# Expert weights worked on during the first batch's attention, in the token tiles' memory

## Chip, cores and metric

The kernel runs on one core of one Trainium2 chip. The metric is the device time of one launch in microseconds (us), lower is better. Engines are called PE (TensorE), DVE (VectorE), ACT (ScalarE), POOL (GpSimd) and SP (SyncE).

## What is computed

Two batches of 2048 tokens of width 256 pass through attention with 4 heads of 64, and then through a layer in which each token goes through one of 8 expert matrices. Cut to what matters:

```python
x = x + _layernorm(attn(_layernorm(x), ln_gamma, ..., w_q, w_k, w_v, w_o, b_o))
# attn: layernorm, q/k/v projections, rmsnorm of q and k, softmax(q k^T) v, w_o
x = x + _layernorm(ffn(_layernorm(x), gate_w, expert_w))

def ffn(x, gate_w, expert_w):
    scores = jnp.einsum('bsh,eh->bse', x, gate_w)
    onehot = jax.nn.one_hot(jnp.argmax(scores, axis=-1), 8)
    expert_out = jnp.einsum('bsh,efh->bsef', x, expert_w)
    return x + jnp.einsum('bsef,bse->bsf', expert_out, onehot)
```

## The kernel before

For each batch there is a front, an attention and an output stage; behind both batches comes the expert stage.

**Front.** 16 token tiles of 128, in groups of 4. Each group gets its statistics (L765, L768) and is normalised (L777) on DVE, transposed on PE (L1191), split into a high and a low part (L481 ACT, L784 DVE) and projected on PE (L1206, L1209, L1154). Then each tile's q and k are squared, summed, scaled and split (L487 and L509 ACT; L788, L796, L799, L807, L815, L818 DVE; L385, L389 POOL) and transposed (L1223, L1226).

**Attention.** 128 steps: 4 heads, 2 blocks of 1024 queries, 16 key tiles. In step s PE makes the scores of 128 keys against 1024 queries (L1300) in one of three PSUM slots; ACT takes the exponential (L574) into one of 6 buffers; POOL issues a DMA that casts it to 16 bits (L412), in most steps (ACT does the cast in one step of 8, at L580, and DVE does the last few); DVE subtracts the cast from the exponential to get the low part (L941); PE multiplies high and low with v (L1318 to L1320), six steps later. PE's order is fixed by hand: the scores of steps k and k+1, then the products of steps k-6 and k-5. The scores of step s wait for the exponential of step s-3, and the exponential of step s for the subtraction of step s-6. Two of the six exponential buffers are the upper half of `x_all`, the memory of the token tiles; its tiles 8 to 15 are therefore loaded again behind the attention (L293), while tiles 0 to 7 stay until the residual (L993).

**Expert weights.** 8 experts by 2 halves of the input features make 16 pieces w of 128 x 256. Each piece passes through four engines: `add_identity` (L354, POOL) adds the identity to its diagonal block, `expert_mean` (L824 and L826, DVE) finds the mean of each row, `high_expert` (L496, ACT) subtracts it and rounds to the high part, and `low_expert` (L360 and L362, POOL) makes the low part. Each waits for the one before it through a semaphore. In this kernel they are loaded in one DMA of 2 MB (L446) into `attn_x1`, the memory that will later take the heads' outputs, and 16 pieces are spread over the first batch's front: piece w is given its mean behind tile w+1, its high part by ACT behind tile w+2, its low part by POOL behind tile w+3. The last mean, the last three high parts and the last three low parts fall into the attention's first eleven steps. `move_out` of the first block waits for all 16 low parts, since it writes `attn_x1`.

**Order.** Every engine runs its own list in program order; a wait at the head holds everything behind it. On ACT, `head_act` runs `exp_step` and then what is hung on the step. On DVE, `head_dve` runs `parts` (the wait for the cast, and L941) and then what is hung on the step. On POOL, what is hung on step s stands ahead of the cast of step s.

Of the kernel before, what the change touches and what calls it, by code (L numbers as in the profile page):

```python
# [6 lines left out]
def build(nc, x, wqkvT, woT, weT, wgT, ln_gamma, ln_beta, q_gamma, k_gamma, b_o, out):  # L7
    f32, f32r, f16, u32 = mybir.dt.float32, mybir.dt.float32r, mybir.dt.float16, mybir.dt.uint32
    ALU, ACT, AX = mybir.AluOpType, mybir.ActivationFunctionType, mybir.AxisListType
    P = 128  # L10
    NB, N, D = x.shape
# [34 lines left out]
    with ExitStack() as ctx:  # L46
# [143 lines left out]

        raw_we = attn_x1[:, 0:KH * NE * D].rearrange("p (k n) -> p k n", k=KH)
        raw_q = q_T[:, :].bitcast(f32)
# [13 lines left out]
        s_rt = [sem(f"s_rt{i}") for i in range(NRT)]  # L206
        s_o = [sem(f"s_o{i}") for i in range(NOT)]
        s_cast = [sem(f"s_cast{i}") for i in range(NHI)]

        s_id, s_ones, s_wf, s_qg, s_q2 = sems("id ones wf qg q2")  # L210

        s_xr, s_tid, s_wI, s_wr, s_wl2 = sems("xr tid wI wr wl2")

# [47 lines left out]
        def dma_casts(s):  # L261
            return not act_casts(s) and not dve_casts(s)

        def casts(by, s):
            return sum(by(i) for i in range(s + 1))
# [7 lines left out]
        def _(sp):  # L273
# [12 lines left out]
            sp.wait_ge(s_tid, TIDS)  # L286
            sp.dma_start(rows_d.rearrange("(s p) w -> p s w", p=P).bitcast(u32), spread(absent[:, :], 1, NSL)).then_inc(s_init, 16)

            for b in range(0, NB):
# [20 lines left out]
        def _(pool):  # L310
# [33 lines left out]
            def half_expert(w):  # L344
                e, k = w // KH, w % KH
                return raw_we[:, k, e * D:(e + 1) * D]

            def add_identity(w):
                k = w % KH
                if w == 0:  # L350
                    pool.wait_ge(s_we, 16)
                    pool.wait_ge(s_id, 4)
                diagonal = half_expert(w)[:, k * P:(k + 1) * P]
                pool.tensor_tensor(diagonal, diagonal, ident[:, :], ALU.add).then_inc(s_wI, 1)  # L354

            def low_expert(w):
                e, k = w // KH, w % KH
                half, cols = half_expert(w), slice(e * D, (e + 1) * D)
                pool.wait_ge(s_weh, w + 1)
                pool.tensor_tensor(half, half, wmean[:, w:w + 1].to_broadcast([P, D]), ALU.add).then_inc(s_wr, 1)  # L360
                pool.wait_ge(s_wr, w + 1)
                pool.tensor_tensor(we_l[:, k, cols], half, we_h[:, k, cols].bitcast(f32), ALU.subtract).then_inc(s_wl2, 1)  # L362
# [15 lines left out]
            for b in range(0, NB):  # L378
                for gi in range(0, NG):
                    for t in range(TG):  # L380
                        n = (b * NG + gi) * TG + t
                        qn = qk_n[t % 2][:, 0:D]
                        qv = qn.rearrange("p (h d) -> p h d", h=H)
                        pool.wait_ge(s_qkn, n + 1)
                        pool.tensor_tensor(qv, qv, spread(gq[:, :], 1, H), ALU.mult).then_inc(s_qg, 1)  # L385
                        pool.wait_ge(s_qg, n + 1)
                        if n > 0:
                            pool.wait_ge(s_qs, n)
                        pool.tensor_tensor(q_sq[:, :], qn, qn, ALU.mult).then_inc(s_q2, 1)  # L389
                        if n == 0:  # L390
                            pool.wait_ge(s_wh, KH + 2)
                            pool.tensor_tensor(wo_l[:, :, 0:D], raw_wo, wo_h[:, :, 0:D].bitcast(f32), ALU.subtract).then_inc(s_wf, 1)
                        if b == 0:
                            add_identity(n)
                        if b == 0 and n >= 3:
                            low_expert(n - 3)
                        if b:
                            scatter_tile(b - 1, n % NT)
                for s in range(b * ALL, (b + 1) * ALL):
                    if 8 <= s < 11:  # L400
                        low_expert(NT - 11 + s)
                    if s == b * ALL + 2:
                        pool.wait_ge(s_T2, b * NT + NT - 1)
                    if s == b * ALL + 3:
                        pool.wait_ge(s_qs, b * NT + NT)
                    if dma_casts(s):
                        pool.wait_ge(s_E, s + 1)
                        if s - NHI + 1 > 0:
                            pool.wait_ge(s_PV, s - NHI + 1)
                        if s < NHI:  # L410
                            pool.wait_ge(s_init, 16)
                        pool.dma_start(high[s % ALL % NHI], whole[s % ALL % NEF]).then_inc(s_cast[s % ALL % NHI], 16)  # L412
# [17 lines left out]
        def _(act):  # L430
# [6 lines left out]
            def prepare():  # L437
# [6 lines left out]
                for k in range(KH):  # L444
                    act.activation(wqkv_h[:, k, 0:3 * D], raw_wqkv[:, k, :], ACT.Copy, scale=gam[:, k:k + 1]).then_inc(s_wh, 1)
                act.dma_start(raw_we, weT.rearrange("(k p) n -> p k n", p=P)).then_inc(s_we, 16)  # L446
                act.wait_ge(s_wgc, 1)
# [23 lines left out]
            for b in range(0, NB):  # L471
# [21 lines left out]
                def high_expert(w):  # L493
                    e, k = w // KH, w % KH
                    act.wait_ge(s_wm, 2 * w + 2)
                    act.activation(we_h[:, k, e * D:(e + 1) * D], raw_we[:, k, e * D:(e + 1) * D], ACT.Identity,  # L496
                                   bias=wmean[:, w:w + 1]).then_inc(s_weh, 1)
# [29 lines left out]
                def a_act(gi, first=False, last=False):  # L527
                    g = b * NG + gi
                    for t in range(TG):
# [9 lines left out]
                        if n == 1:  # L539
                            gate_of_output()  # L540
                        if b == 0 and 2 <= n < NT - 1:
                            high_expert(n - 2)
                        if t == 2 and not last:
# [41 lines left out]
                def head_act(b, h):  # L585
                    hh = b * H + h
                    for k in range(STEPS):
# [4 lines left out]
                        if h == 0 and k == 1:  # L592
                            move_k(end - 1, NT - 1)
                        if b == 0 and h == 0 and k in (5, 6, 7):
                            high_expert(NT - 8 + k)

# [90 lines left out]
        def _(dve):  # L687
# [73 lines left out]
            for b in range(0, NB):  # L761
# [59 lines left out]
                def expert_mean(w):  # L821
                    e, k = w // KH, w % KH
                    dve.wait_ge(s_wI, w + 1)
                    dve.tensor_reduce(wesum[:, w:w + 1], raw_we[:, k, e * D:(e + 1) * D], AX.X, ALU.add).then_inc(s_wm, 1)  # L824
                    dve.wait_ge(s_wm, 2 * w + 1)
                    dve.tensor_scalar(wmean[:, w:w + 1], wesum[:, w:w + 1], -1.0 / D, None, ALU.mult).then_inc(s_wm, 1)  # L826

                def a_dve(gi, first=False, last=False):
                    g = b * NG + gi
                    for t in range(TG):  # L830
# [5 lines left out]
                        if n == 1:  # L836
                            gate_of_output()
                        if b == 0 and n >= 1:
                            expert_mean(n - 1)
                        if not (first and t < 1):  # L840
# [102 lines left out]
                def move_out(h, qb):  # L943
                    unit = (b * H + h) * NQB + qb
                    dve.wait_ge(s_PV, unit * NT + NT)
                    if unit == b * H * NQB and b:
                        dve.wait_ge(s_sc, b * NT * 16)
                    if unit == 0:
                        dve.wait_ge(s_wl2, NE * KH)
                    inverse = rl[:, unit % 2, :].rearrange("p (b q) -> p b q", b=2)  # L950
# [6 lines left out]
                def head_dve(b, h):  # L957
                    hh = b * H + h
                    for k in range(STEPS):
# [5 lines left out]
                        if h == 0 and k == 0:  # L965
                            largest_out(1)
                        if b == 0 and h == 0 and k == 2:
                            expert_mean(NT - 1)
                        if h == 0 and k == 4:
# [15 lines left out]
                def residual(i):  # L985
                    pr = b * NP + i
                    dve.wait_ge(s_r1, pr + 1)
                    dve.reciprocal(rs1[:, i % 2, :], sd1[:, i % 2, :]).then_inc(s_k1, 1)
                    dve.wait_ge(s_k1, pr + 1)
                    if 2 * i == XT:  # L990
                        dve.wait_ge(s_xr, (b + 1) * (NEF - 4) * 16)
# [479 lines left out]
```

## Time and profile before

| | us |
|---|---|
| median of 3 runs | 762.37 |
| lowest, highest | 761.49, 763.06 |
| profiled execution | 765.08 |
| its span, first to last instruction | 763.4 |
| front of batch 0, up to its first exponential | 0 to 108.9 |
| attention of batch 0, up to the last block's move | 108.9 to 314 |
| first exponential of batch 1 | 435.5 |

A line of the trace names an instruction's place in the code (L574), its engine, what it writes and reads, how many there were, and its times. What stands in brackets, or behind a bar, is the time that the engine was idle just before, and what ended it.

### The profile page before, as it was taken

To read this page: it belongs to the slowest core of one execution; us is meant where nothing else is said; L and a number is where in the kernel's file an instruction comes from. 1 tells how busy PE (TensorE), PEld (TensorE's weight loads), DVE (VectorE), ACT (ScalarE), POOL (GpSimd) and SP (SyncE) were. 2 spreads that over 40 slices of the span, in tenths; PEclk is the share of its full clock that TensorE was granted. 3 is DMA by queue.
4 is the path that set the end of the run, shared out by engine and by line. 5 is a ranking of instruction groups with operands and counts; after the bars stand their busy time and mean duration, and the time that the engine had idled before them with its cause. 6 is when DMAs were issued, how large, how long until landed. Compare 5 with 4: busy or idle time off the path is not lost.

```text
span 763.4 us, 22051 instructions
## 1 busy us (share of the span) xinstructions
PE 656.3 (86%) x8914; PEld 447.4 (59%) x8914; DVE 607.0 (80%) x1169; ACT 538.4 (71%) x866; POOL 271.9 (36%) x454
## 2 busy tenths in 40 slices
PE   4988878999999999867999899999999998706882
PEld 2666544566666656755766556666666567505772
DVE  4799978878887888896887777888887888963884
ACT  3278788888888878582677988888888785713552
POOL 2245565232332322000555622323323220071775
PEclk9589999999999999996898899999999999956997
DMA  7910006997979878121000178879798781024551
GB/s 251 270 37 1 1 17 113 169 162 142 166 144 163 154 144 151 57 69 44 29 29 22 45 133 156 161 141 167 145 163 153 141 153 58 3 96 135 175 164 44
DMA packets 53815, 87.13 MB, mean 114 GB/s; under 512 B 6608, under 2 KB 23250, under 8 KB 53460
## 3 DMA queue, kind: packets, MB, share of 16 engines
q0 software_dynamic: 34848, 65.61, 44.7%
q1 hardware_dynamic: 18020, 18.03, 8.4%
q10 hardware_dynamic: 848, 2.10, 0.8%
q8 instruction: 71, 1.16, 0.7%
q14 instruction: 28, 0.23, 0.1%
HBM read 14.82 MB, written 14.79 MB: 39 GB/s over the span
## 4 chain that ended last, share of the span: by engine, by line
PE 50%; DVE 22%; DMA 10%; ACT 8%; issue 7%; POOL 1%; SPq 0%; POOLq 0%; DVEq 0%; ACTq 0%
PE banks L1300 13%; PE banks L1154 12%; DVE e_l L941 6%; PE banks L1318 5%; DMA e_h<-e_f 5%; PE banks L1319 5%; PE banks L1206 4%; PE banks L1320 4%; DMA e_x<-x_all 4%; ACT e_f L574 2%; DVE x_all L993 1%; PE banks L1191 1%; PE banks L1422 1%; PE banks L1209 1%; ACT x_all L574 1%
## 5 line engine op out<-in xcount | busy, mean ns | idle before, releaser
L941 DVE TENSOR_TENSOR e_l<-e_f,e_h 128x1024 f16<-128x1024 f32 x172 | 207.7, 1230 | 40.5 <-DMA e_h<-e_f 37.5
L574 ACT ACTIVATE e_f<-banks,nbias,c_ 128x1024 f32<-128x1024 f32 x172 | 199.0, 1200 | 44.6 <-PE banks L1300 44.6
L1300 PE MATMUL banks<-q_T,k_T 128*128 128x512 f16 (+1 forms) x1024 | 204.5, 384 | 4.8 <-DVE e_l L807 3.2
L1320 PE MATMUL banks<-v_mm,e_l 128*128 128x65 f16 x2048 | 201.8, 191 | 0.0
L1320 PEld LDWEIGHTS banks<-v_mm,e_l 128*128 128x128 f16 x2048 | 189.6, 99 | 0.0
L1318 PEld LDWEIGHTS banks<-v_mm,e_h 128*128 128x128 f16 x1376 | 126.0, 96 | 44.2 <-issue 24.9
L1318 PE MATMUL banks<-v_mm,e_h 128*128 128x65 f16 x1376 | 136.7, 193 | 9.2 <-DVE e_l L941 4.3
L412 POOL DMA_DIRECT2D e_h<-e_f x148 | 78.5, 530 | 175.7 <-ACT e_f L574 170.1
L1319 PE MATMUL banks<-v_mm,e_h 128*128 128x64 f16 x1376 | 136.2, 195 | 0.0
L1319 PEld LDWEIGHTS banks<-v_mm,e_h 128*128 128x128 f16 x1376 | 127.2, 97 | 0.0
L941 DVE TENSOR_TENSOR e_l<-x_all,e_x 128x1024 f16<-128x1024 f32 x84 | 101.7, 1227 | 21.2 <-DMA e_x<-x_all 17.7
L574 ACT ACTIVATE x_all<-banks,nbias,c_ 128x1024 f32<-128x1024 f32 x84 | 97.5, 1201 | 21.3 <-PE banks L1300 19.9
L1300 PEld LDWEIGHTS banks<-q_T,k_T 128*128 128x128 f16 (+1 forms) x1024 | 55.9, 96 | 94.3 <-issue 58.0
L1318 PEld LDWEIGHTS banks<-v_mm,e_x 128*128 128x128 f16 x672 | 61.5, 96 | 20.2 <-issue 11.0
L1318 PE MATMUL banks<-v_mm,e_x 128*128 128x65 f16 x672 | 66.9, 193 | 2.7 <-DVE attn_x L955 1.8
L1319 PE MATMUL banks<-v_mm,e_x 128*128 128x64 f16 x672 | 66.6, 195 | 0.0
L412 POOL DMA_DIRECT2D e_x<-x_all x70 | 37.0, 528 | 82.0 <-ACT x_all L574 73.9
L1319 PEld LDWEIGHTS banks<-v_mm,e_x 128*128 128x128 f16 x672 | 62.1, 97 | 0.0
L385 POOL TENSOR_TENSOR e_l<-e_l,gq 128x256 f32<-128x256 f32 x32 | 28.5, 889 | 87.9 <-DVE e_l L807 87.9
L426 POOL DMA_INDIRECT out<-k_T x40 | 39.5, 988 | 30.4 <-DVE k_T L1135 23.1
L487 ACT ACTIVATE e_f<-banks 128x512 f32<-128x512 f32 x32 | 19.1, 596 | 33.3 <-PE banks L1154 30.3
L374 POOL DMA_INDIRECT rows_d<-attn_x,rowat x32 | 31.8, 994 | 29.0 <-DVE ttab L1082 18.2
(268 smaller groups left out, 1237.4 us busy)
## 6 DMA issues: line engine op xcount, KB each, us to landing
e_h<-e_f POOLq DMA_DIRECT2D x148, 256.0 KB, 3.9
e_x<-x_all POOLq DMA_DIRECT2D x70, 256.0 KB, 4.0
x_all<-x SPq DMA_DIRECT2D x12, 512.0 KB, 4.4
rows_d<-e_x SPq DMA_DIRECT2D x1, 5180.0 KB, 24.4
k_T<-rows_d SPq DMA_DIRECT2D x20, 259.0 KB, 3.1
attn_x<-weT ACTq DMA_DIRECT2D x1, 2048.0 KB, 7.6
q_T<-wqkvT SPq DMA_DIRECT2D x1, 768.0 KB, 6.2
out<-k_T POOLq DMA_INDIRECT x40, 2.7
```

The lines of the kernel that those rows point to most:

```text
L374: pool.indirect_dma_start(out=rows_d, out_offset=bass.IndirectOffsetOnAxis(ap=rowat[:, b * NT + i:b * NT + i + 1], axis=0), in_=x1_all[:, ...
L385: pool.tensor_tensor(qv, qv, spread(gq[:, :], 1, H), ALU.mult).then_inc(s_qg, 1)
L412: pool.dma_start(high[s % ALL % NHI], whole[s % ALL % NEF]).then_inc(s_cast[s % ALL % NHI], 16)
L426: pool.indirect_dma_start(out=out_rows, out_offset=bass.IndirectOffsetOnAxis(ap=rt[q % NRT][:, t, D + 2:D + 3].bitcast(u32), axis=0), in_= ...
L574: act.activation(whole[s % ALL % NEF], ps_S[s % ALL % 3], ACT.Exp, bias=bias_of(h, k // NT), scale=CESC).then_inc(s_E, 1)
L941: dve.tensor_tensor(low[s % ALL % NLO], whole[s % ALL % NEF], high[s % ALL % NHI], ALU.subtract).then_inc(s_El, 1)
L1154: ins = pe.matmul(dst, l, r, start=(i == 0), stop=(i == n - 1))
L1206: pe.matmul(ps_QK[t % 2], l, r, start=i == 0, stop=False)
L1300: ins = pe.matmul(ps_S[s % ALL % 3][:, c * BANK:(c + 1) * BANK], k_T[rows, 1 - c if cross else c, h * N + j * P:h * N + (j + 1) * P], q_T[ ...
L1318: pe.matmul(o, high[s % ALL % NHI][:, at], v[:, 0:DH + 1], start=first, stop=False, skip_group_check=True)
L1319: pe.matmul(o[:, 0:DH], high[s % ALL % NHI][:, at], v[:, DH + 1:VW], start=False, stop=False, skip_group_check=True)
L1320: ins = pe.matmul(o, low[s % ALL % NLO][:, at], v[:, 0:DH + 1], start=False, stop=j == NT - 1, skip_group_check=True)
```

## The change

The expert weights move out of `attn_x1` and out of the front. `x_all[:, 0:8]` has been normalised for the first batch by then, and nobody reads it until the residual. It takes experts 0 to 3 (two DMAs by SP, issued once eight tiles have been normalised), then experts 4 to 7 one by one as places come free, and then the eight token tiles again, one by one (eight DMAs), before the first residual, which waits for them. The work on piece w is hung on steps of the first batch's attention: with s = 4 + 7w, POOL adds the identity ahead of the cast of step s; DVE makes the mean behind the subtraction of step s; ACT makes the high part behind the exponential of step s+2; POOL makes the low part in two halves, ahead of the casts of steps s+4 and s+5. The ACT-issued load of 2 MB and `move_out`'s wait for the low parts are gone.

```diff
-        raw_we = attn_x1[:, 0:KH * NE * D].rearrange("p (k n) -> p k n", k=KH)
+        WSLOTS = NT // 2 // KH
+        raw_we = x_all[:, 0:KH * WSLOTS, :].rearrange("p (k e) d -> p k e d", k=KH)
...
+        def expert_at(s):
+            first, every = 4, 7
+            if s >= first and (s - first) % every == 0 and (s - first) // every < NE * KH:
+                return (s - first) // every
+            return None
...
+            weT_k = weT.rearrange("(k p) (e d) -> p k e d", p=P, d=D)
+            sp.wait_ge(s_xh, KH * WSLOTS)
+            for k in range(KH):
+                sp.dma_start(raw_we[:, k], weT_k[:, k, 0:WSLOTS]).then_inc(s_we, 16)
+            for e in range(WSLOTS, NE):
+                sp.wait_ge(s_wl2, KH * (e - WSLOTS + 1))
+                sp.dma_start(raw_we[:, :, e - WSLOTS, :], weT_k[:, :, e]).then_inc(s_wx[e - WSLOTS], 16)
+            for e in range(WSLOTS, NE):
+                sp.wait_ge(s_wl2, KH * (e + 1))
+                for k in range(KH):
+                    at = k * WSLOTS + e - WSLOTS
+                    sp.dma_start(x_all[:, at, :], x_d[:, at, :]).then_inc(s_xw, 16)
...
             def add_identity(w):
-                k = w % KH
+                e, k = w // KH, w % KH
+                if e < WSLOTS:
+                    pool.wait_ge(s_we, 16 * KH)
+                else:
+                    pool.wait_ge(s_wx[e - WSLOTS], 16)
...
                 pool.tensor_tensor(half, half, wmean[:, w:w + 1].to_broadcast([P, D]), ALU.add).then_inc(s_wr, 1)
+
+            def lowest_expert(w):
+                e, k = w // KH, w % KH
+                half, cols = half_expert(w), slice(e * D, (e + 1) * D)
                 pool.wait_ge(s_wr, w + 1)
                 pool.tensor_tensor(we_l[:, k, cols], half, we_h[:, k, cols].bitcast(f32), ALU.subtract).then_inc(s_wl2, 1)
...
-                        if b == 0:
-                            add_identity(n)
-                        if b == 0 and n >= 3:
-                            low_expert(n - 3)
...
-                    if 8 <= s < 11:
-                        low_expert(NT - 11 + s)
+                    for part, lag in ((add_identity, 0), (low_expert, 4), (lowest_expert, 5)):
+                        w = expert_at(s - lag)
+                        if w is not None:
+                            part(w)
...
-                act.dma_start(raw_we, weT.rearrange("(k p) n -> p k n", p=P)).then_inc(s_we, 16)
...
-                        if b == 0 and 2 <= n < NT - 1:
-                            high_expert(n - 2)
...
-                        if b == 0 and h == 0 and k in (5, 6, 7):
-                            high_expert(NT - 8 + k)
+                        if expert_at(hh * STEPS + k - 2) is not None:
+                            high_expert(expert_at(hh * STEPS + k - 2))
...
-                        if b == 0 and n >= 1:
-                            expert_mean(n - 1)
...
-                    if unit == 0:
-                        dve.wait_ge(s_wl2, NE * KH)
...
-                        if b == 0 and h == 0 and k == 2:
-                            expert_mean(NT - 1)
+                        if expert_at(hh * STEPS + k) is not None:
+                            expert_mean(expert_at(hh * STEPS + k))
...
+                    if pr == 0:
+                        dve.wait_ge(s_xw, KH * WSLOTS * 16)
```

## Rows read from the trace of the kernel before

**Rows 1.** The page: busy us and share of each engine; granted clock in 40 slices
```profile
PE 656.3 (86%) x8914; PEld 447.4 (59%) x8914; DVE 607.0 (80%) x1169; ACT 538.4 (71%) x866; POOL 271.9 (36%) x454
...
PEclk9589999999999999996898899999999999956997
```
**Rows 2.** Busy time by stretch: us, PE, PEld, DVE, ACT, POOL, clock, DMA share, GB/s
```profile
32.00:42.00 10.00, 10.00 (x42) 7.28 (x43) 6.80 (x18) 4.82 (x13) 2.50 (x4) 0.64 0.96 239
...
45.70:106.60 60.90, 50.60 (x329) 36.22 (x328) 58.43 (x142) 48.91 (x113) 36.39 (x60) 0.97 0.00 1
...
376.30:433.20 56.90, 52.71 (x329) 38.29 (x328) 47.02 (x118) 43.98 (x102) 32.35 (x36) 0.91 0.08 27
...
377.50:383.86 6.36, 4.81 (x40) 3.56 (x39) 5.82 (x20) 4.69 (x13) 3.86 (x5) 1.00 0.06 21
383.86:387.28 3.42, 3.42 (x10) 2.00 (x7) 3.35 (x9) 2.49 (x6) 0.87 (x2) 0.50 0.00 0
...
404.30:411.20 6.90, 6.90 (x29) 5.17 (x28) 4.62 (x13) 4.28 (x11) 3.35 (x4) 0.51 0.12 41
...
149.61:246.41 96.80, 95.37 (x1794) 60.59 (x1792) 79.09 (x76) 80.28 (x73) 29.56 (x56) 1.00 0.85 154
```
**Rows 3.** Groups of instructions in batch 0's front, 45.7 to 106.6 us: busy, mean ns
```profile
L824 DVE TENSOR_REDUCE wesum<-attn_x 128x1 f32<-128x256 f32 x12 | 4.9, 408 | 0.0
...
L815 DVE TENSOR_TENSOR e_l<-e_l 128x512 f16<-128x512 f32 x6 | 6.1, 1017 | 0.0
...
L777 DVE TENSOR_SCALAR e_h<-x_all,mv,rs 128x256 f32<-128x256 f32 x8 | 5.3, 728 | 0.1
...
L496 ACT ACTIVATE we_h<-attn_x,wmean 128x256 fp32r<-128x256 f32 x11 | 5.5, 499 | 0.0
```
**Rows 4.** The same groups in batch 1's front, 376.3 to 433.2 us
```profile
L815 DVE TENSOR_TENSOR e_l<-e_l 128x512 f16<-128x512 f32 x6 | 4.1, 680 | 0.0
...
L777 DVE TENSOR_SCALAR e_h<-x_all,mv,rs 128x256 f32<-128x256 f32 x8 | 3.4, 481 | 0.1
```
**Rows 5.** One line's instructions: durations ns min/median/max; the casts' landing below L412
```profile
L354 POOL TENSOR_TENSOR attn_x<-attn_x,ident x16: 454/458/508, 29.5 to 109.7; 128x128 f32<-128x128 f32 x16
...
L362 POOL TENSOR_TENSOR we_l<-attn_x,we_h x16: 722/726/1601, 50.3 to 130.7; 128x256 fp32r<-128x256 f32 x16
...
L360 POOL TENSOR_TENSOR attn_x<-attn_x,wmean x16: 607/613/1032, 49.6 to 129.6; 128x256 f32<-128x256 f32 x16
...
L412 POOL DMA_DIRECT2D e_x<-x_all x70: 527/527/565, 119.0 to 618.6; - x70
...
DMA to landing us min/median/max: 2.8/4.0/5.7
```
**Rows 6.** Exponentials counted in stretches: us, ACT busy (count), clock, DMA share, GB/s
```profile
149.60:246.40 96.80, 73.50 (x64) 1.00 0.85 154
108.90:124.60 15.70, 9.38 (x8) 0.89 0.57 104
124.60:136.80 12.20, 9.21 (x8) 1.00 0.64 117
435.50:450.00 14.50, 9.01 (x8) 0.78 0.63 118
```
**Rows 7.** Timeline, ACT, POOL and DVE: one step of the attention (step 33)
```profile
162.62 1.05 ACT L580 ACTIVATE e_h<-e_f 128x1024 f16<-128x1024 f32 x1
163.57 1.19 ACT L574 ACTIVATE e_f<-banks,nbias,c_ 128x1024 f32<-128x1024 f32 x1
164.66 2.29 ACT L574 ACTIVATE x_all<-banks,nbias,c_ 128x1024 f32<-128x1024 f32 x2
167.47 2.30 ACT L574 ACTIVATE e_f<-banks,nbias,c_ 128x1024 f32<-128x1024 f32 x2 [0.52 <-PE banks L1300]
...
165.06 0.53 POOL L412 DMA_DIRECT2D e_h<-e_f  x1 [1.46 <-ACT e_f L574]
...
169.44 1.22 DVE L941 TENSOR_TENSOR e_l<-e_f,e_h 128x1024 f16<-128x1024 f32 x1 [1.13 <-DMA e_h<-e_f]
```
**Rows 8.** Timeline, where the last pieces lie in batch 0's attention today
```profile
120.53 0.41 DVE L824 TENSOR_REDUCE wesum<-attn_x 128x1 f32<-128x256 f32 x1
120.97 0.15 DVE L826 TENSOR_SCALAR wmean<-wesum 128x1 f32<-128x1 f32 x1
...
122.78 0.50 ACT L496 ACTIVATE we_h<-attn_x,wmean 128x256 fp32r<-128x256 f32 x1
123.17 1.19 ACT L574 ACTIVATE e_f<-banks,nbias,c_ 128x1024 f32<-128x1024 f32 x1
...
127.45 1.60 POOL L362 TENSOR_TENSOR we_l<-attn_x,we_h 128x256 fp32r<-128x256 f32 x1
...
128.38 6.10 DVE L941 TENSOR_TENSOR e_l<-e_f,e_h 128x1024 f16<-128x1024 f32 x4
```
**Rows 9.** Who waited for whom, 136 to 290 us: total us, times, longest
```profile
ACT e_f L574 <- PE banks L1300: 18.2, 25, 1.9
...
DVE e_l L941 <- DMA e_h<-e_f: 15.7, 16, 1.8
```
**Rows 10.** Timeline of the start: ACT's load of the weights, SP's store of empty rows
```profile
9.51 0.39 ACTq L446 DMA_DIRECT2D attn_x<-weT  x1
...
18.73 0.51 SPq L287 DMA_DIRECT2D rows_d<-e_x  x1
```
**Rows 11.** The page: DMA issues, KB each, us to landing
```profile
rows_d<-e_x SPq DMA_DIRECT2D x1, 5180.0 KB, 24.4
...
attn_x<-weT ACTq DMA_DIRECT2D x1, 2048.0 KB, 7.6
```
**Rows 12.** Timeline, DVE: the first residual of batch 0
```profile
319.00 0.88 DVE L993 SCALAR_TENSOR_TENSOR x_all<-banks,rs,x_all 128x256 f32<-128x256 f32 x2
```

More of the change, by code:

```diff
@@ L207, in build @@
         s_o = [sem(f"s_o{i}") for i in range(NOT)]
+        s_wx = [sem(f"s_wx{i}") for i in range(NE // 2)]
         s_cast = [sem(f"s_cast{i}") for i in range(NHI)]
         s_id, s_ones, s_wf, s_qg, s_q2 = sems("id ones wf qg q2")
-        s_xr, s_tid, s_wI, s_wr, s_wl2 = sems("xr tid wI wr wl2")
+        s_xr, s_xw, s_tid, s_wI, s_wr, s_wl2 = sems("xr xw tid wI wr wl2")
         s_prep, s_const, s_ws, s_woc, s_wgc, s_bc, s_wm, s_b2, s_bq, s_wl = sems("prep const ws woc wgc bc wm b2 bq wl")
@@ L345, in half_expert @@
                 e, k = w // KH, w % KH
-                return raw_we[:, k, e * D:(e + 1) * D]
+                return raw_we[:, k, e % WSLOTS, :]
             def add_identity(w):
-                k = w % KH
+                e, k = w // KH, w % KH
[3 more added lines that the diff above has]
+                    pool.wait_ge(s_wx[e - WSLOTS], 16)
                 if w == 0:
-                    pool.wait_ge(s_we, 16)
                     pool.wait_ge(s_id, 4)
@@ L495, in high_expert @@
                     act.wait_ge(s_wm, 2 * w + 2)
-                    act.activation(we_h[:, k, e * D:(e + 1) * D], raw_we[:, k, e * D:(e + 1) * D], ACT.Identity,
+                    act.activation(we_h[:, k, e * D:(e + 1) * D], raw_we[:, k, e % WSLOTS, :], ACT.Identity,
                                    bias=wmean[:, w:w + 1]).then_inc(s_weh, 1)
@@ L823, in expert_mean @@
                     dve.wait_ge(s_wI, w + 1)
-                    dve.tensor_reduce(wesum[:, w:w + 1], raw_we[:, k, e * D:(e + 1) * D], AX.X, ALU.add).then_inc(s_wm, 1)
+                    dve.tensor_reduce(wesum[:, w:w + 1], raw_we[:, k, e % WSLOTS, :], AX.X, ALU.add).then_inc(s_wm, 1)
                     dve.wait_ge(s_wm, 2 * w + 1)
```

## Prediction

> **What bounds the kernel now.** I read the page first: PE is busy 86%, DVE 80%, ACT 71% [rows 1]. That is an average over stages, so the next view is the busy time by stretch. In batch 0's front, from 45.7 to 106.6 us (tiles 3 to 15), DVE is busy 58.4 of 60.9 us and PE 50.6: DVE sets the pace there. The same twelve tiles of batch 1 take 56.9 us with DVE busy only 47.0 [rows 2]; batch 1 has no expert pieces, so it is a measured picture of batch 0's front without them. Before that, at 32 to 42 us, PE is busy 10.0 of 10 us at a clock of 0.64 and DVE 6.8 [rows 2], so nothing taken from DVE helps there. In the attention PE is busy 95.4 of 96.8 us [rows 2]; 64 exponentials start in these 96.8 us [rows 6], which is 1.51 us a step and 10.6 us for seven. DVE and ACT are busy 79 and 80 us of it. They have room on average; what matters for this change is the order in which they meet, so the last view is the timeline of one step.
>
> **The front.** Removed per piece on DVE: L824 0.41 and L826 0.15 us, 0.56 in sequence [rows 3, 8]; on ACT L496 0.50; on POOL three operations. Beside it, what is left becomes shorter: L815 takes 1.02 us in batch 0 and 0.68 in batch 1, and L777 0.73 and 0.48 [rows 3, 4], where POOL works on no pieces. Twelve pieces give 6.7 us of DVE time, the L815 rows 2.0 and L777 2.0: some 10.7 of 58.4, more than the path can give back, since PE and ACT come next. The bounds come from batch 1: 60.9 - 56.9 = 4.0 us as measured. But batch 1's stretch has 10.3 us at a clock of 0.5 (two stretches [rows 2]), in which PE did half the work, and batch 0's 3.4 us; the difference of 6.9 us at half speed is 3.5 us, which makes 7.5. The three tiles before may add up to 3.1 (their time over that of batch 1's, in a stretch that PE fills): 10.6 at most. I take **-6.5**, between 4.0 and 10.6 and nearest to 7.5, since the clock may fall in the new front as in batch 1's.
>
> **The start.** The 2 MB load at 9.51 us [rows 10] goes. The transfers that the start waits for have landed by then, and later ones are needed long after: 0 us. The new load of 1 MB stands on SP's queue behind the 5180 KB store [rows 10], issued at 18.7 us and landing 24.4 us later, so at 43; with 7.6 us for twice as much [rows 11] it is there by about 50, and step 4 comes after 108: 0 us. If the cover were gone, it would cost its landing time, at most 7.6.
>
> **The attention, order of work.** This is the step that decides. Take the trace of step 33 [rows 7]: its exponential ends at 164.76; POOL issues the cast at 165.06; it has landed when DVE starts L941 at 169.44, which ends at 170.66. The exponential of step 36, three steps later, starts at 167.47. So DVE finishes a step 5.9 us after its exponential, and by then ACT has been at the exponential of step s+3 for 3.2 us. The change hangs the mean on DVE behind L941 of step s, and lets ACT, behind the exponential of step s+2, wait for this mean. ACT waits in order: behind that wait stand L496 and the exponentials of all later steps, and behind those PE's scores, POOL's casts and in the end DVE itself. The wait cannot be met in time in any step for which POOL issues the cast.
>
> From the end of the exponential of step s to the start of that of step s+3:
> - 0.3 to the cast's issue [rows 7], 4.0 from there to its landing (2.8 at the least, 5.7 at most [rows 5]), 1.2 for L941 [rows 7];
> - 0.6 for L824 and L826; L496 starts and is through 0.4 later, as far as the next exponential is concerned (122.78 to 123.17) [rows 8].
>
> Sum 6.5, against 3.3 on average today (three steps less one exponential of 1.2). Then come the exponentials of steps s+3 to s+7, as fast as ACT can: four starts 1.1 apart and 1.2 for the last [rows 7], 5.6 us, and half of ACT's cast of 1.05 every eight steps: 0.5. Step s+7 is the next s. One round is 6.5 + 5.6 + 0.5 = 12.6 us; I add 0.3 because in every other round PE can't give the scores of s+7 that early (it must do two products between pairs of scores), and 0.4 for POOL's pieces: 13.3, against 10.6. **+2.7 a round.** For 15 rounds (pieces 1 to 15): 40.5. PE can't win this back between stalls, since its 95.4 of 96.8 us are its own work. Nor can casts run ahead, since the same stall holds them.
>
> Piece 0 takes the place of the last mean, three high and three low parts, which lie in the first steps now; batch 0's first eight steps took 15.7 us and batch 1's 14.5 [rows 6]. A gain of 1 and a charge of about 1: 0.
>
> Bounds of a round: with landings of 2.8 and none of the additions 6.5 - 1.2 + 5.6 + 0.5 = 11.4, or +0.8; with 5.7, 15.0, or +4.4. For 15 rounds +12 to +66. I take 4.0 because DMA share is 0.85 today [rows 2], and ACT's exponentials, and so the casts, come in bursts 1.1 apart after each stall.
>
> **POOL's pieces.** L354 0.46, L360 0.61 and L362 0.73 us alone [rows 5] are 1.8 us a round on an engine that is busy 29.6 of 96.8 us [rows 2]. What they do to others shows where they lie in the attention now: L362 stretches to 1.60 and four L941 take 6.10 us instead of 4.9 [rows 8], 0.3 each. Once or twice a round, that is the 0.4 above. The Trainium skill (SBUF — State Buffer, Who interferes with whom) says that a DVE instruction with two SBUF inputs and a GpSimd instruction that reads SBUF shut each other out for the whole of an instruction. By that rule a round could lose up to 1.8 us on DVE, where the row has 0.3 an instruction; on the path, fifteen times 1.8 would add 27 us, and I follow the row.
>
> **Clock.** In batch 1's front the clock went to 0.5 at 383.86, after a stretch in which PE was busy 4.81 of 6.36 us, or 76% [rows 2]. In the new rounds PE is busy 10.5 of 13.3 us, or 79%, so falls are likely. Each of 3.4 us costs PE 1.7 us of work, but most of that lies in PE's own new idle time. Between 0 and 13 (eight falls, fully paid) I take **+4**.
>
> **The rest.** Twelve loads, 2 MB in all, run beside the casts; alone 2 MB took 7.6 us [rows 11], the bound of their cost; their effect is within the landing that I took: 0. `add_identity` stands ahead of the cast of step s while POOL still waits for the exponential: 0. SP's own queue: the reloads of tiles 8 to 15 and the next batch's tiles now stand behind the last low part at step 114; they wait for step 124 anyway: 0. The first residual at 319.0 [rows 12] waits for tiles whose last load is issued about step 114, some 28 us earlier, and takes about 4: 0, and at most 4 without cover. `move_out`'s lost wait was met at step 11, before step 18: 0.
>
> **Sum.** -6.5 + 40.5 + 4 = +38. The profiled execution took 765.1, which would become 803.1; it stands 2.7 above the median of the runs, so on their scale 762.4 + 38 = **800.4**.
>
> **Rivals.**
> - *The stall is mostly caught up.* Landings near 2.8 (the queue is empty after a stall) and no clock falls: -10.6 + 12 gives 764, and from there to 776. For it: two of three PSUM slots can be full when ACT resumes. Against: casts in a burst queue. 8%.
> - *Faster.* Buffers absorb the wait. ACT waits for PE 18.2 us in 154 in one of its two groups alone [rows 9]; if this room and the three PSUM slots carried ACT over, only the front's gain would stay: 762.4 - 6.5 = 755.9. It decides if the mean is there within about 2 us of the end of the exponential of s+2, and the row says 3 or more. The Trainium skill (Perfetto Trace Analysis, Optimization Strategy) says that where the most-contended engine changes over time, interleaving the regimes may help; by that rule DVE work would leave a front that DVE bounds for an attention that PE bounds, for this same 756. The rows of busy time agree with it, the timeline of order does not. 6%.
> - *The clock stays down* for much of the attention. At half speed a round of PE's own work takes 21 us instead of 10.6; over a quarter of the rounds that is +40 more, 840. 6%.
> - *Forecast*, one stall a round: 80%.
>
> **How the numbers follow.** The forecast's own ends are 776 (rounds at +1.3, the front at -6.5, no clock cost) and 828 (rounds at +4.4, the front at -4, the clock at +4); the range is these, with 8% below, 6% faster and 6% above left out. What a measurement can tell from no change is 0.2%, 1.5 us. Faster by more: 6%. Within 0.2%: 2%, out of the first rival. Slower: 92%.
>
> **What would show it.** In the profile after, ACT's L496 should have idle time before it, some 3 us, fifteen times, ended by DVE's L826; L574's wait for PE should shrink; PE should have new idle time at L1300, ended by ACT's L574; exponentials should come in bursts of four or five 1.1 us apart with a gap behind them; a stretch of 64 should take about 122 us instead of 96.8. The front of batch 0 should reach its first exponential near 102 instead of 108.9, with L815 at 0.68 us. L496 without idle time before it, or the exponentials still 1.51 apart, would prove the forecast wrong; a residual that waits for a DMA would be a mistake in the part on the rest.

## The result

The change is slower: 802.9 us (798.6 to 808.1) against 762.7 (761.5 to 765.2); the ratio is 1.051, with an interval of 1.047 to 1.055. The forecast was 800.4. The profiled execution took 804.7 us, with a span of 803.0.

Line numbers have moved: L574 is now L597 (exponential), L941 L962 (subtraction), L412 L438 (cast), L1300 L1321 (scores), L1318 to L1320 L1339 to L1341 (products), L496 L521 (high part), L824 and L826 L847 and L849 (mean), L354, L360 and L362 L378, L384 and L390 (POOL's pieces), L815 L838, L777 L800.

The start times of the first exponential and of that of step 120 in each batch cut the two executions into stages (us; "behind" is everything behind batch 1's step 120):

| | to first exponential | batch 0's attention | between | batch 1's attention | behind |
|---|---|---|---|---|---|
| before | 108.9 | 186.5 | 140.1 | 184.5 | 143.4 |
| the change | 99.2 | 236.6 | 139.5 | 184.6 | 143.1 |
| difference | -9.7 | +50.1 | -0.6 | +0.1 | -0.3 |

The whole loss is in the first batch's attention. Busy time in this stage, before and (second row) in the change (us, PE, PEld, DVE, ACT, POOL, clock, DMA share, GB/s):

```profile
108.90:295.37 186.47, 178.70 (x3243) 110.89 (x3239) 152.48 (x159) 153.48 (x143) 64.11 (x115) 0.99 0.82 149
```

```profile
99.16:335.70 236.54, 195.70 (x3234) 118.26 (x3231) 161.38 (x187) 158.41 (x155) 92.14 (x154) 0.92 0.68 126
```

The page of the profile after, its clock row and the groups that changed:

```profile
PE 671.5 (84%) x8914; PEld 453.4 (56%) x8914; DVE 602.6 (75%) x1169; ACT 537.9 (67%) x866; POOL 284.8 (35%) x454
...
PEclk9699988999999999999599889999999999965997
...
L1321 PE MATMUL banks<-q_T,k_T 128*128 128x512 f16 (+1 forms) x1024 | 214.2, 394 | 41.5 <-ACT e_f L597 26.9
...
L521 ACT ACTIVATE we_h<-x_all,wmean 128x256 fp32r<-128x256 f32 x16 | 8.1, 508 | 53.3 <-DVE wmean L849 53.3
```

The last row says it in one line: 16 high parts, 8.1 us of work, and 53.3 us in which ACT stood still for the means. DVE and ACT do no more work in all than they did [rows 1]. Who waited for whom in the changed attention, 108 to 330 us (total us, times, longest):

```profile
ACT we_h L521 <- DVE wmean L849: 53.3, 16, 5.4
...
PE banks L1321 <- ACT e_f L597: 26.4, 17, 4.2
DVE e_l L962 <- DMA e_x<-x_all: 17.7, 14, 3.7
ACT e_f L597 <- PE banks L1321: 16.1, 15, 2.2
...
DVE e_l L962 <- PE banks L1341: 13.9, 7, 2.9
```

In [rows 9] ACT waited for PE. It still does, but less (22.6 us in both its groups over this stage, 31.6 before), and now PE waits for ACT, at the scores. One such round, as the chain of waits goes through it (start, us, what):

```profile
205.01 0.52 POOL x_all L378
205.53 5.73 DMA e_x<-x_all
...
211.35 1.23 DVE e_l L962
212.58 0.34 DVE wesum L847
...
212.94 0.17 DVE wmean L849
...
213.54 1.19 ACT e_f L597
```

And the same moment in the timelines of ACT and PE:

```profile
205.88 2.30 ACT L597 ACTIVATE e_f<-banks,nbias,c_ 128x1024 f32<-128x1024 f32 x2 [0.68 <-PE banks L1321]
213.13 0.51 ACT L521 ACTIVATE we_h<-x_all,wmean 128x256 fp32r<-128x256 f32 x1 [4.95 <-DVE wmean L849]
213.54 1.19 ACT L597 ACTIVATE e_f<-banks,nbias,c_ 128x1024 f32<-128x1024 f32 x1
...
214.78 1.59 PE L1321 MATMUL banks<-q_T,k_T 128*128 128x512 f16 x6 [3.74 <-ACT e_f L597]
```

This is step 53, whose exponential ended at 205.20. ACT has finished the exponential of step 55 at 208.18 and can do nothing until the mean behind step 53's subtraction is there. PE has filled its three slots and stands for 3.7 us. It is the chain that the forecast drew from step 33 [rows 7]: exponential, cast, subtraction, mean, high part, next exponential.

### The profile page after: what moved, and what is told of

Read it like the earlier page. It is cut to its first block, busy times and chain, and to the rows that moved or that the text cites. A ratio compares the mean times of both kernels' runs of the same rounds, so it can differ in the third digit from the quotient of the medians.

```text
span 803.0 us, 22064 instructions
## 1 busy us (share of the span) xinstructions
PE 671.5 (84%) x8914; PEld 453.4 (56%) x8914; DVE 602.6 (75%) x1169; ACT 537.9 (67%) x866; POOL 284.8 (35%) x454
## 4 chain that ended last, share of the span: by engine, by line
PE 32%; DVE 18%; DMA 12%; ACT 10%; issue 9%; POOL 2%; POOLq 0%; ACTq 0%; DVEq 0%
PE banks L1175 9%; DVE e_l L962 9%; PE banks L1321 8%; DMA e_h<-e_f 7%; DMA e_x<-x_all 4%; ACT e_f L597 4%; PE banks L1339 3%; PE banks L1227 3%; PE banks L1340 3%; PE banks L1341 2%; ACT x_all L597 2%; DVE x_all L1014 1%; PE banks L1443 1%; ACT e_h L603 1%; PE banks L1247 1%
## 5 line engine op out<-in xcount | busy, mean ns | idle before, releaser
L962 DVE TENSOR_TENSOR e_l<-e_f,e_h 128x1024 f16<-128x1024 f32 x172 | 210.2, 1244 | 64.9 <-DMA e_h<-e_f 49.1
L1321 PE MATMUL banks<-q_T,k_T 128*128 128x512 f16 (+1 forms) x1024 | 214.2, 394 | 41.5 <-ACT e_f L597 26.9
L597 ACT ACTIVATE e_f<-banks,nbias,c_ 128x1024 f32<-128x1024 f32 x172 | 198.8, 1199 | 39.3 <-PE banks L1321 39.3
L1341 PE MATMUL banks<-v_mm,e_l 128*128 128x65 f16 x2048 | 209.5, 194 | 0.0
L1341 PEld LDWEIGHTS banks<-v_mm,e_l 128*128 128x128 f16 x2048 | 194.1, 101 | 0.0
L1339 PEld LDWEIGHTS banks<-v_mm,e_h 128*128 128x128 f16 x1376 | 128.5, 97 | 42.0 <-issue 27.8
L1339 PE MATMUL banks<-v_mm,e_h 128*128 128x65 f16 x1376 | 141.1, 195 | 6.3 <-DVE e_l L962 4.3
L438 POOL DMA_DIRECT2D e_h<-e_f x148 | 79.5, 537 | 188.2 <-ACT e_f L597 178.5
L1340 PE MATMUL banks<-v_mm,e_h 128*128 128x64 f16 x1376 | 140.6, 197 | 0.0
L1321 PEld LDWEIGHTS banks<-q_T,k_T 128*128 128x128 f16 (+1 forms) x1024 | 55.5, 97 | 140.1 <-issue 62.7
L1340 PEld LDWEIGHTS banks<-v_mm,e_h 128*128 128x128 f16 x1376 | 129.8, 98 | 0.0
L962 DVE TENSOR_TENSOR e_l<-x_all,e_x 128x1024 f16<-128x1024 f32 x84 | 103.3, 1249 | 31.4 <-DMA e_x<-x_all 25.9
L597 ACT ACTIVATE x_all<-banks,nbias,c_ 128x1024 f32<-128x1024 f32 x84 | 97.6, 1199 | 18.4 <-PE banks L1321 17.0
L1339 PEld LDWEIGHTS banks<-v_mm,e_x 128*128 128x128 f16 x672 | 63.4, 98 | 19.7 <-issue 13.1
L413 POOL TENSOR_TENSOR e_l<-e_l,gq 128x256 f32<-128x256 f32 x32 | 34.7, 1086 | 108.5 <-DVE e_l L830 108.5
L1339 PE MATMUL banks<-v_mm,e_x 128*128 128x65 f16 x672 | 70.0, 196 | 1.5 <-DVE attn_x L974 1.2
L1340 PE MATMUL banks<-v_mm,e_x 128*128 128x64 f16 x672 | 69.7, 198 | 0.0
L438 POOL DMA_DIRECT2D e_x<-x_all x70 | 37.5, 535 | 86.6 <-ACT x_all L597 78.7
L1340 PEld LDWEIGHTS banks<-v_mm,e_x 128*128 128x128 f16 x672 | 64.0, 99 | 0.0
L452 POOL DMA_INDIRECT out<-k_T x40 | 39.6, 991 | 30.1 <-DVE k_T L1156 22.4
L521 ACT ACTIVATE we_h<-x_all,wmean 128x256 fp32r<-128x256 f32 x16 | 8.1, 508 | 53.3 <-DVE wmean L849 53.3
## 6 DMA issues: line engine op xcount, KB each, us to landing
x_all<-weT SPq DMA_DIRECT2D x2, 512.0 KB, 12.3
```

The lines of the kernel that those rows point to most:

```text
L452: pool.indirect_dma_start(out=out_rows, out_offset=bass.IndirectOffsetOnAxis(ap=rt[q % NRT][:, t, D + 2:D + 3].bitcast(u32), axis=0), in_= ...
L597: act.activation(whole[s % ALL % NEF], ps_S[s % ALL % 3], ACT.Exp, bias=bias_of(h, k // NT), scale=CESC).then_inc(s_E, 1)
L962: dve.tensor_tensor(low[s % ALL % NLO], whole[s % ALL % NEF], high[s % ALL % NHI], ALU.subtract).then_inc(s_El, 1)
L1321: ins = pe.matmul(ps_S[s % ALL % 3][:, c * BANK:(c + 1) * BANK], k_T[rows, 1 - c if cross else c, h * N + j * P:h * N + (j + 1) * P], q_T[ ...
L1339: pe.matmul(o, high[s % ALL % NHI][:, at], v[:, 0:DH + 1], start=first, stop=False, skip_group_check=True)
L1340: pe.matmul(o[:, 0:DH], high[s % ALL % NHI][:, at], v[:, DH + 1:VW], start=False, stop=False, skip_group_check=True)
```

## The experiments

The stage that they are read from is batch 0's attention, from its first exponential to that of step 120: 186.5 us before, 236.6 in the change. Each is one profiled execution; the unchanged copy of the kernel before took 187.4, and a second profile of the kernel with ACT's part at s+6 took 190.0 where the first had 188.7. So a difference of about 1 us in this stage tells nothing. Every time of a whole kernel is compared with runs of the kernel before on the same chip. The experiments ran in three series, each on a chip of its own. On two of these chips the kernel before itself took 780 to 781 us, on the third 763.8: its unchanged copy on one of the two had nearly the same stages up to batch 1's step 120 (620.3 us in all, against 620.0), and the expert stage took 160.8 in place of 143.4.

**1. Take ACT's wait away, leave everything else.**

```diff
                 pool.wait_ge(s_weh, w + 1)
+                pool.wait_ge(s_wm, 2 * w + 2)
...
-                    act.wait_ge(s_wm, 2 * w + 2)
+                    act.wait_ge(s_wI, w + 1)
...
-                                   bias=wmean[:, w:w + 1]).then_inc(s_weh, 1)
+                                   bias=eps[:, 0:1]).then_inc(s_weh, 1)
```

> All instructions of the change stay; ACT's high part no longer waits for DVE's mean (it takes a constant as bias and waits for POOL's identity only, so the experts are not centred). Theory A (the cost is ACT's in-order wait for a mean that stands behind the cast): the stall goes, the attention of batch 0 from its first exponential to that of step 120 falls from 236.5 us back to 187 to 195, and with the front's 9.7 us gained the whole takes 753 to 762 us. Rival B (the cost is the added work of DVE and POOL on shared engines and the loads beside the casts): the attention stays above 215 us and the whole above 782. Rival C (the clock's falls are a cause of their own): the falls stay at about one in 27 us and the whole is near 785.

Ratio to before 1.011 (1.001 to 1.020), where A had expected a kernel no slower than before. Busy time from the first exponential to that of step 120 (us, PE, PEld, DVE, ACT, POOL, clock, DMA share, GB/s):

```profile
101.72:303.65 201.93, 180.53 (x3235) 111.76 (x3233) 169.21 (x186) 159.72 (x155) 102.34 (x154) 0.99 0.79 147
```

ACT's wait cost 34.7 us (236.6 to 201.9), most of the loss. But 15.4 us were left, where A had expected 8.5 at the most, so A as stated fell short. B's floor of 215 is not reached either. C is refuted as a cause of its own: with the stall gone the clock fell once in this stage, for 3.4 us, in place of nine times. The waits of this run, whose lines stand one further down, name the rest:

```profile
POOL x_all L385 <- DVE wmean L850: 26.6, 12, 5.3
```

With ACT no longer held, POOL gets to its low part (step s+4) before the mean is there; it now stands still, up to 5.3 us, with casts behind it. The same wait has moved to another engine.

**2. Take both waits away.** ACT as above; POOL takes the constant too, and the wait that experiment 1 gave it is not there. DVE's two instructions stay, on a finished weight.

```diff
-                pool.tensor_tensor(half, half, wmean[:, w:w + 1].to_broadcast([P, D]), ALU.add).then_inc(s_wr, 1)
+                pool.tensor_tensor(half, half, eps[:, 0:1].to_broadcast([P, D]), ALU.add).then_inc(s_wr, 1)
...
-                    dve.tensor_reduce(wesum[:, w:w + 1], raw_we[:, k, e % WSLOTS, :], AX.X, ALU.add).then_inc(s_wm, 1)
+                    dve.tensor_reduce(wesum[:, w:w + 1], wo_h[:, k, 0:D].bitcast(f32), AX.X, ALU.add).then_inc(s_wm, 1)
```

> As the run without ACT's wait, and POOL doesn't wait for the mean either: DVE's two mean instructions stay but read a finished weight, ACT and POOL take a constant (the experts are not centred). All positions and amounts of work are those of the change. Theory A, refined (in order waits for the mean are the cost on ACT and on POOL, where the low part of step s+4 stands ahead of a cast): batch 0's attention from its first exponential to that of step 120 takes 187 to 192 us, where the run without ACT's wait had 201.9 and the one with everything six steps later 188.7. Rival B (where POOL's pieces lie, right ahead of casts four and five steps on, disturbs by itself): it stays at 198 to 202.

```profile
99.28:288.04 188.76, 178.63 (x3234) 111.19 (x3231) 169.11 (x188) 158.74 (x155) 98.45 (x154) 0.99 0.85 158
```

188.8 us, and a ratio of 0.992 (0.987 to 0.997): a little faster than before. All the work of the change, at its places, with its loads and reloads, costs some 2 us; the waits for the mean, with everything that follows from them, the clock's falls included, cost the other 48. B is out.

**3. Only move POOL's parts, four steps later (s+8 and s+9).**

```diff
-                    for part, lag in ((add_identity, 0), (low_expert, 4), (lowest_expert, 5)):
+                    for part, lag in ((add_identity, 0), (low_expert, 8), (lowest_expert, 9)):
```

> The change with ACT as it is (step s+2, with its wait) and POOL's two halves moved from s+4 and s+5 to s+8 and s+9. If the two waits cost apart (ACT 34.7 of the 50.1 us, POOL 13.2), batch 0's attention falls from 236.6 to 222 to 226 us. If ACT's stall alone sets the rounds, since POOL's wait is met by then anyway (ACT resumes only when the mean is there), it stays at 233 to 237 us.

```profile
101.98:343.20 241.22, 196.30 (x3233) 117.96 (x3230) 167.72 (x188) 158.62 (x156) 100.50 (x154) 0.92 0.66 123
```

241.2 us, ratio 1.061 (1.050 to 1.071): no gain. The two waits don't add. In the change POOL never waits for the mean: no such line is in its view of waits. Its wait appears, and costs 13.1 us (201.9 less 188.8), only once ACT's is gone. That it is 4.6 us over the change's 236.6 was not expected; each is one profiled execution, and I did not follow it up.

**4. Make the same work wait for nothing: a longer distance.** In each, ACT's part is hung on step s+L, and POOL's on s+L+2 and s+L+3. This one is L = 6:

```diff
-                    for part, lag in ((add_identity, 0), (low_expert, 4), (lowest_expert, 5)):
+                    for part, lag in ((add_identity, 0), (low_expert, 8), (lowest_expert, 9)):
...
-                        if expert_at(hh * STEPS + k - 2) is not None:
-                            high_expert(expert_at(hh * STEPS + k - 2))
+                        if expert_at(hh * STEPS + k - 6) is not None:
+                            high_expert(expert_at(hh * STEPS + k - 6))
```

> The same with ACT's high part at step s+6 and POOL's halves at s+8 and s+9. Theory A: ACT reaches the wait 9.0 us after the exponential of step s, later than every mean seen: no stall, exponentials of seven steps in 10.6 to 11.2 us, whole 753 to 762 us, so at or below the kernel before. Rival B: 795 or more.

> ACT's high part is hung on step s+4 in place of s+2, POOL's two halves on s+6 and s+7; nothing else. Theory A: the mean is there 5.7 to 7.9 us after the end of the exponential of step s, and ACT reaches the wait after 6.0 us in place of 3.0, so a stall of 0 to 2 us is left in a part of the rounds: 765 to 778 us. Rival B: the work is the same, so the time stays within 5 us of 803.

> ACT's high part at step s+3, POOL's halves at s+5 and s+6. The stretch from batch 0's first exponential to that of step 120 took 236.6 us at s+2, 202.0 at s+4 and 188.7 at s+6. If a round costs what the mean is late (step s+3 gives ACT one exponential, 1.2 us, and one step's distance of 1.5 us more, 15 times): 236.6 less 18 to 23, so 214 to 219 us. If the cost were one of having the wait at all, whatever its distance: 230 or more.

| ACT's part at step | attention, us | idle before the 16 high parts, us | ratio to before |
|---|---|---|---|
| s+2 (the change) | 236.6 | 53.3 | 1.051 |
| s+3 | 211.7 | 37.6 | 780.3 us against 763.8, one execution |
| s+4 | 202.0 | 24.5 | 1.016 (1.009 to 1.022) |
| s+6 | 188.7, again 190.0 | 0 | 0.994 (0.991 to 0.998) |

The row of s+6:

```profile
102.02:290.72 188.70, 178.43 (x3238) 111.08 (x3235) 170.04 (x187) 158.54 (x156) 99.78 (x154) 0.99 0.85 157
```

POOL never waits for the mean in these three, so the table shows ACT's wait alone. One step is worth 24.9 us, the next 9.7: the cost falls with the distance, and B's "same time within 5 us" is refuted again. At s+3 the stretch ended a little below the expected 214 to 219. At s+4 the whole kernel was 12 us slower than before, so 776 on the scale of 763.8: inside the 765 to 778 expected. At s+6 the wait is always met, and the calculation is complete again: this kernel is faster than the kernel before and than the change. The same kernel once more, on another chip:

> The kernel with ACT at s+6 again, for its time alone. By the stages of the profiles it gains 7.4 us in the front and gives back 2 in the attention: 5.4 us, a ratio of 0.993; 0.994 was measured. If that was chance, the ratio is 0.998 or more.

Ratio 0.994 (0.991 to 0.997): 759.2 us against 763.8. Both intervals lie below 1, so the gain of 4.6 us is clear of noise, though small.

**5. What do the pieces disturb when nobody waits?** The kernel of L = 6 without POOL's low parts; the loads into freed places then wait for the high parts.

```diff
-                    for part, lag in ((add_identity, 0), (low_expert, 8), (lowest_expert, 9)):
+                    for part, lag in ((add_identity, 0),):
```

> The kernel with ACT at s+6, without POOL's low parts (L384, L390 left out; the expert stage takes the high weights in their place). If POOL's instructions hold up DVE's subtraction, its mean in batch 0's attention falls from 1.357 us to below 1.26, and the stretch from 188.7 to 186 to 187 us. If it is the mean and the identity that cost, it stays at 188 to 189.

Subtractions of batch 0's attention, with the low parts and (second fence) without (busy us, mean ns, idle before):

```profile
L962 DVE TENSOR_TENSOR e_l<-e_f,e_h 128x1024 f16<-128x1024 f32 x78 | 103.7, 1365 | 8.2 <-DMA e_h<-e_f 7.0 <-PE banks L1341 0.9
...
L390 POOL TENSOR_TENSOR we_l<-x_all,we_h 128x256 fp32r<-128x256 f32 x16 | 17.3, 1080 | 0.5
```

```profile
L962 DVE TENSOR_TENSOR e_l<-e_f,e_h 128x1024 f16<-128x1024 f32 x78 | 94.8, 1245 | 13.4 <-DMA e_h<-e_f 13.0
```

The subtraction falls from 1.37 to 1.25 us (1.39 in the second profile at s+6). POOL's operations do hold DVE up, 0.12 us on the mean of 116 subtractions or 14 us in all, but DVE has room for most of that: the stretch took 187.1 us, 1.6 and 2.9 less than the two profiles at s+6. That is little more than these two differ by themselves, and the ratios of the whole overlap (0.989, 0.981 to 0.996, against 0.994), so how much reaches the path is not shown.

**6. The front.** The kernel before, once without the means and once without the low parts. What would have read them takes a constant, or the high weights, and waits for the step ahead of them instead.

```diff
-                        if b == 0 and n >= 1:
-                            expert_mean(n - 1)
```

> The kernel before without its 16 means on DVE (a constant in their place, the experts are not centred). It tells how the front's 9.7 us divide. If DVE's own two instructions carry the gain: first exponential of batch 0 at 101 to 103 us in place of 108.9. If the gain is mostly from POOL's operations no longer disturbing DVE (L815 0.68 in place of 1.02, L777 0.48 in place of 0.73 us): 104 to 107.

```diff
-                        if b == 0 and n >= 3:
-                            low_expert(n - 3)
```

> The kernel before without POOL's low parts (L360, L362; the expert stage takes the high weights in their place). Tiles 3 to 15 of batch 0's front take 60.9 us with everything, 58.0 without the means and 53.5 without any piece. If POOL's operations hold up DVE (L777 0.69 us in place of 0.56): 58 to 59.5 us. If POOL's low parts cost the front nothing, since DVE's own two instructions and ACT's high part are what the path sees: 60.5 to 61.

Tiles 3 to 15 took 60.9 us before, 58.0 without the means, 58.7 without the low parts and 53.5 in the change (the first two of the four rows of busy time are the change and the kernel of L = 6):

```profile
43.30:96.80 53.50, 49.66 (x329) 36.23 (x328) 46.84 (x117) 43.77 (x102) 20.77 (x24) 0.97 0.00 1
```

```profile
46.10:99.60 53.50, 49.72 (x329) 36.05 (x328) 46.87 (x117) 43.82 (x102) 20.77 (x24) 0.97 0.00 1
```

```profile
43.50:101.50 58.00, 52.78 (x329) 38.59 (x328) 47.89 (x117) 48.69 (x113) 41.20 (x60) 0.91 0.00 1
```

```profile
45.80:104.50 58.70, 51.59 (x329) 37.57 (x328) 55.14 (x141) 48.78 (x113) 21.21 (x36) 0.94 0.00 1
```

2.9 and 2.2 us make 5.1 of the 7.4, if they add, which was not tried; both single runs had a lower clock than the two with 53.5, and ACT's high part and the identity are gone only in the change, so the other 2.3 us are not divided. The first exponential came at 103.8 without the means (101 to 103 or 104 to 107 had been written down, so it fell between the two), at 106.8 without the low parts, and at 109.0 in the unchanged copy:

> The kernel before, unchanged, for a second profile of it. First exponential of batch 0 at 106 to 109 us, depending on how long the clock stays at 0.5 behind 22 us (17.1 us in the first profile, 13.7 in that of the change); batch 0's attention 186 to 187 us. If the first exponential is near 106.5 with 13.7 us at the lower clock, some 2.5 of the 9.7 us that the front seemed to gain are the clock's and not the change's.

The copy had 17.1 us at a clock of 0.5 from 22.2 us on, like the first profile, and tile 3 at 45.8 (45.7 in the first). The change's profile had 13.7 (20.7 to 34.3), and its tile 3 came at 43.3 us. The front of the change was profiled nine times in all, with the later parts of the kernel varied: four times the clock stayed down for 13.7 us, and the first exponential came at 99.1 to 99.9; five times it stayed down for 17.1, and it came at 101.6 to 102.0. So of the 9.7 us in the table at the top 7.4 are the change's, and 2.3 belong to the start of that one execution: the clock was down 3.4 us less (1.7 us of work at half speed), and 0.7 us was ahead by the second group's statistics (23.1 us in place of 23.8). The run without the means had 13.7 us as well, so its 103.8 compares with some 106.5 and not with 108.9.

## Why the prediction was right

- **The whole.** The forecast was +38; the two profiled executions differ by 39.6 and the medians by 40.2. It was near by its mechanism. Part of the nearness is luck: the attention's loss was 5.6 us larger than forecast, the front's gain 0.9 larger, and the profiled execution had 2.3 us from its start.
- **The front: -6.5 forecast.** 7.4 measured between the same tiles, against a best estimate of 7.5 from batch 1's front corrected for the clock. The stated bounds (4.0 to 10.6) held. L838 took 0.68 us and L800 0.48, as in [rows 4].
- **One cause in that part was wrong.** I put L815's 1.02 us down to POOL's pieces. Without the low parts it was still 0.93; without the means, with all of POOL's pieces left, 0.68. (L777, the other one, took 0.73 us before, 0.53 without the low parts and 0.59 without the means: there POOL's pieces do count, though not alone.) The timelines of DVE and POOL say why. Before, and (second fence) without the means:

```profile
51.92 0.41 DVE L824 TENSOR_REDUCE wesum<-attn_x 128x1 f32<-128x256 f32 x1
52.36 0.15 DVE L826 TENSOR_SCALAR wmean<-wesum 128x1 f32<-128x1 f32 x1
52.43 0.92 DVE L815 TENSOR_TENSOR e_l<-e_l 128x512 f16<-128x512 f32 x1
...
52.08 0.72 POOL L385 TENSOR_TENSOR e_l<-e_l,gq 128x256 f32<-128x256 f32 x1 [1.06 <-DVE e_l L807]
```

```profile
49.35 0.68 DVE L815 TENSOR_TENSOR e_l<-e_l 128x512 f16<-128x512 f32 x1
...
49.51 1.10 POOL L385 TENSOR_TENSOR e_l<-e_l,gq 128x256 f32<-128x256 f32 x1 [1.48 <-DVE e_l L807]
```

  The mean's two instructions let POOL's product L385 start first, and L815 behind them was held; without them L815 starts first and L385 is held, 1.10 for 0.72 us. The Trainium skill (SBUF — State Buffer, SBUF: two separate sides) says that of a DVE instruction with two inputs in SBUF and a GpSimd instruction that reads SBUF, as L815 and L385 are, whichever starts first has the shared pair of ports for its whole instruction. These two pairs of rows agree in kind: the second to start is the one that takes longer.
- **The attention: one stall a round, +2.7 forecast.** From the start of the exponential of step 11 (120.28) to that of step 116 (329.75) are 15 rounds in 209.5 us, 13.96 each; before they took 10.70 (128.88 to 289.39). So +3.26 a round, 49 us, where the forecast had 40.5 and 4 for the clock. Two terms were too small. The time from the end of an exponential to the end of its subtraction is 5.5 in the sum and 5.9 on the mean of the fifteen steps that carry a piece, 0.4 a round; step 33 in [rows 7] had 5.9 already. Landings weren't longer (2.8, 3.7 and 6.1 us, in place of 2.8, 4.0 and 5.7 [rows 5]). In the 13 of these steps whose cast is POOL's, DVE started 0.3 us behind the landing, most of it in a few steps where it was still busy with an earlier subtraction. In the other two (steps 39 and 95) ACT makes the cast, a case that the forecast left out, and the subtraction ended 7.0 and 6.7 us behind the exponential. The rest, 0.3 a round, lies behind the stall: from the start of the exponential of step s+3 to the end of that of s+7 took 7.1 us on the mean, where the sum has 6.8 (5.6 and 0.5, and the 0.3 and 0.4 added). ACT ran these as fast as it can (5.6 us) in four rounds of fifteen; the others took 6.5 to 9.1. What I had not drawn is that DVE also waits for PE to free a low buffer, 13.9 us in seven waits, which was 1.6 before. That PE is late with its products because it was held at its scores is my reading; I did not try that apart.
- **POOL's pieces: 0.4 a round.** No row shows this on the path. Subtractions took 1.27 us on the mean against 1.24 before, some 0.2 us a round, and those in the chain 1.22, as in the sum. That the 0.4 did no harm to the total is luck. What the forecast did not see is another cost of the same pieces, POOL's wait for the mean: it does not appear in the change, and experiment 1 shows that it costs 13 us in all when ACT's is gone.
- **Clock: +4.** The clock did go to 0.5 in the changed attention, nine times (twice for 6.8 us, seven times for 3.4), where it had gone once before. The first fall, at 99.2, lies ahead of any round. Around each of the other eight PE had stood still at its scores for 2.0 to 4.2 us, and the standstill ended at most 1.2 us before the fall or was still going on. At s+4, with half the idle time, it fell at the start alone. What the falls cost by themselves was not measured, and 4 may be too low. PE was busy 195.7 us where it had been busy 178.7 for the same matmuls, so the falls added up to 17 us to its work, some of it in time in which PE would have stood idle. And a microsecond of ACT's wait cost 0.63 us at s+4 (one fall) and 0.67 at s+3 (two), but 0.94 in the change (nine). At 0.65 the change's 53.3 us would have cost 35; by this estimate up to 15 of the 50 us came with the falls, or with other effects of a longer stall. No run separates them.
- **The rest at 0** held: the stages between and behind agree within 0.6 us, the weights were issued at 29.3 us and landed in 12.3, and the residual did not wait for a DMA.
- **The rivals.** Faster, 755.9, the one that the rule of the Trainium skill (Perfetto Trace Analysis, Optimization Strategy) also gives: not as it was made. But with the wait out of the way it did come out faster, by 4.6 us (0.6%), of the 6.5 which that rival had. So the runs at s+6 agree with the rule and the change does not: it speaks of the work and not of its order. The caught-up stall and the clock that stays down (a quarter of the rounds at half speed) didn't come; the clock was at 0.5 for 37.5 of 236.6 us.

## What to carry to other kernels

When small work is hung on the steps of a pipeline, compare its distance with the latency of the chain that it crosses, not with how busy the engines are: here a subtraction ends some 6 us, or 4 steps of 1.5 us, behind its exponential, so a part that waits for what stands behind it stalled at 2, 3 and 4 steps' distance and not at 6. The same 16 pieces cost 50 us at two steps and some 2 us at six. If an in-order wait is removed and less comes back than expected, look for the engine that now reaches the same semaphore next.

## What the runs showed of the hardware

- Two engines can trade a delay without any change to either: 0.24 us on DVE's L815 became 0.38 us on POOL's L385 when the mean's two instructions on DVE ahead of L815 went.
- With the front's code unchanged, its first exponential came at 99.1 to 99.9 us in four executions, in which the clock stayed at 0.5 for 13.7 us from 20.6 to 21.7 us on, and at 101.6 to 102.0 in five, in which it stayed there for 17.1 us from 21.9 to 22.8 us on. In the changed attention the falls from 160.6 on lay 27.3 us apart (187.9, 215.2, 242.5), about two rounds of 13.96; whether the rounds set this spacing was not tried.
- The same kernel before took 143.4 us behind batch 1's step 120 on one chip and 160.8 on another, all other stages being equal within 1 us. Over all profiled executions this stage took 156 to 161 us on two of the chips and 141 to 143 on the third and in the two executions of the result, whatever the kernel, so it goes with the chip or with the series. Its cause is open.
